# Moving the expert input products to even steps, regrouping the last steps' picks, and scattering the last three halves by quarters in a one-core Trainium2 kernel

## The reference, cut to what matters

```python
x = layernorm(x + attn(x))            # x: 4 x 1024 x 128, attn: gates and a scan over the sequence
# ffn, for all 4096 tokens; h = 8 heads, nk = 32 keys a side, k = 8, ne = 1024 experts
xn = (x - mu) * rsqrt(var + eps) * gamma + beta        # over the batch
q = xn @ w_q.T;  sim = einsum('pbnhd,hkpd->pbnhk', q, keys)
s, i = top_k(sim, 8)                                   # for x and for y
scores, pk = top_k(all pairs sx + sy, 8);  idx = take(ix * nk + iy, pk)
o = einsum('bnd,bnhkd->bnhk', inputs, key_in[idx])
o = gelu(o) * softmax(scores)
out = layernorm(x + einsum('bnhk,bnhkd->bnd', o, key_out[idx]))
```

## Time and profile before

| | |
|---|---|
| median of 3 runs | 500.65 us (500.22 to 504.22) |
| the profiled execution, in full | 502.43 us |
| its span, first to last instruction | 500.6 us |
| mean granted TensorE clock in it | 0.788 |
| DVE busy | 429.3 us (86%) |
| PE busy | 364.9 us (73%) |
| POOL busy | 255.0 us (51%) |
| ACT busy | 243.7 us (49%) |

### The profile page before, as it was taken

One profiled execution on the slowest core, in us unless ns is written; L12 is line 12 of the kernel. 1 busy time (PEld: TensorE's weight loads), 2 busy tenths in 40 slices (PEclk: granted clock), 3 DMA queues, 4 the chain that ended last, 5 costly groups with the idle time before them and its releaser, 6 DMA issues.

```text
span 500.6 us, 24184 instructions
## 1 busy us (share of the span) xinstructions
PE 364.9 (73%) x10097; PEld 266.1 (53%) x10097; DVE 429.3 (86%) x2691; ACT 243.7 (49%) x398; POOL 255.0 (51%) x345
## 2 busy tenths in 40 slices
PE   5979855266738787787877778778787778778755
PEld 3445542024433657375647554665467366737745
DVE  2457986999999889999999999999999999994922
ACT  2897664346324533563474437353654572344222
POOL 1023350552549465658747473769294938474600
PEclk9989956668556887887797679867987887878769
DMA  8800000000000000000000000000000000000001
GB/s 237 187 1 1 1 1 0 2 0 5 3 4 3 3 4 5 3 3 7 26 1 5 25 5 2 5 25 4 3 5 27 2 5 4 26 1 5 25 5 44
DMA packets 7662, 8.96 MB, mean 18 GB/s; under 512 B 896, under 2 KB 6912, under 8 KB 7424
## 3 DMA queue, kind: packets, MB, share of 16 engines
q1 hardware_dynamic: 6976, 7.34, 5.4%
q10 hardware_dynamic: 576, 0.07, 0.1%
HBM read 5.31 MB, written 2.10 MB: 15 GB/s over the span
## 4 chain that ended last, share of the span: by engine, by line
PE 39%; DVE 22%; issue 13%; POOL 10%; ACT 3%; ACTq 0%; DVEq 0%; POOLq 0%
PE psum L904 15%; PE psum L880 11%; PE psum L891 7%; PE psum L860 5%; DVE vals L625 4%; POOL arena L295 4%; DVE picked L658 3%; DVE idx L633 3%; DVE arena L689 3%; DVE arena L685 2%; POOL ixf L258 2%; DVE arena L682 2%; POOL code L263 1%; DVE top L639 1%; ACT arena L444 1%
## 5 line engine op out<-in xcount | busy, mean ns | idle before, releaser
L880 PE MATMUL psum<-arena 64*64 64x16 f16 x8192 | 93.6, 180 | 69.2 <-issue 60.9
L880 PEld LDWEIGHTS psum<-arena 64*64 64x64 f16 x8192 | 85.8, 116 | 87.7 <-issue 77.3
L904 PE MATMUL psum<-ko,arena 64*128 64x128 f32 x1024 | 90.4, 354 | 3.3 <-issue 3.3
L904 PEld LDWEIGHTS psum<-ko,arena 64*128 64x128 f32 x1024 | 87.0, 265 | 4.2 <-issue 3.8
L633 DVE FIND_INDEX8 idx<-vals,sims 128x8 uint32<-128x32 f32 x512 | 82.6, 186 | 0.0
L295 POOL TENSOR_TENSOR arena<-arena 128x512 f32<-128x512 f32 x60 | 77.3, 1318 | 4.8 <-ACT arena L436 4.8
L891 PE MATMUL psum<-x1T,trn 128*64 128x256 f32 x512 | 66.3, 412 | 13.8 <-ACT arena L444 13.7
L685 DVE TENSOR_TENSOR arena<-iota,listsT 128x4096 f16<-128x4096 f16 x32 | 76.3, 2385 | 0.0
L436 ACT ACTIVATE arena<-psum 128x1024 f32<-128x1024 f32 x32 | 32.6, 1018 | 67.8 <-PE psum L880 67.8
L891 PEld LDWEIGHTS psum<-x1T,trn 128*64 128x64 f32 x512 | 35.5, 148 | 51.5 <-ACT arena L444 25.8
L243 POOL TENSOR_TENSOR cand<-vals 128x128 f32<-128x128 f32 x16 | 9.4, 588 | 95.5 <-DVE vals L625 95.5
(11 more groups left out here) (118 smaller groups left out, 573.7 us busy)
## 6 DMA issues: line engine op xcount, KB each, us to landing
x<-in_L_attn_x_dram SPq DMA_DIRECT2D x8, 256.0 KB, 5.7
out_dram<-nat SPq DMA_DIRECT2D x7, 256.0 KB, 2.2
ko<-in_L_ffn_key_out_dram SPq DMA_DIRECT2D x2, 512.0 KB, 8.7
nat<-in_L_ffn_key_in_dram SPq DMA_DIRECT2D x2, 256.0 KB, 9.2
nat<-in_L_ffn_keys_dram SPq DMA_DIRECT2D x2, 128.0 KB, 5.6
out_dram<-nat SPq DMA_DIRECT2D x2, 128.0 KB, 1.7
nat<-in_L_attn_W_delta_dram SPq DMA_DIRECT2D x1, 64.0 KB, 2.9
nat<-in_L_attn_W_in_dram SPq DMA_DIRECT2D x1, 64.0 KB, 2.8
```

The source lines that it names most:

```text
L880: end = pe.matmul(psum[64 * e:64 * e + 64, at:at + NJ], hotx[rows, g, :, e], hotw[rows, part, g, :, e], start=(part == 0), stop=(part == 1))
L904: end = pe.matmul(y2[:, e, m % 2] if m < NS - 1 else y_last[:, e], gl[rows, m % 4, j, :], ko[rows, j, :], start=(j == 0), stop=(j == NJ - 1))
```

## The change

- `experts_in(q)` and `gelus(q)` run in step 2q and no longer in step 2q + 1 (`GELU_STEP`). In step 0 the Gelus stand ahead of `exps(0)`, `low_halves(0)` and `signs(0)`. In the other even steps `signs(m)` stands ahead of the third Gelu. The Gelu buffer `gl` has six slots for four.
- On DVE the `hots_of` of step 14 are taken out of step 15's body. After the loop stand `residual(5)`, `hots_of(14, 0)`, the statistics, the whole pick of step 15, `hots_of(14, 1)`, `hots_of(15, 0)`, `scales`, `hots_of(15, 1)`.
- The last three halves, (14, 1), (15, 0) and (15, 1), are scattered by `quarters`: 128 matmuls a half with 32 columns, the high and the low part side by side and no longer added in PSUM. ACT copies a quarter's low part out (`low_out`), DVE adds the high part (`both_parts`) and multiplies with the Gelus; for step 14's first half POOL does so in four short products after the last one-hots.
- `experts_out(13)` is issued before the last three halves.

```diff
+    GL = 6
+    GELU_STEP = tuple(range(0, NS, 2))
...
-        arena = sb("arena", [P, 24576])
+        arena = sb("arena", [P, 25600])
...
-        gl = arena[:, at_gl:at_gl + 4 * AW].rearrange("p (u j w) -> p u j w", u=4, j=NJ)
+        gl = arena[:, at_gl:at_gl + GL * AW].rearrange("p (u j w) -> p u j w", u=GL, j=NJ)
...
+        LAST = 2 * NS - 3
+        quarter_base = (0, 4, 2)
+
+        def quarter(u, part):
+            m, hf, b = (LAST + u // 2) // 2, (LAST + u // 2) % 2, u % 2
+            at = slice(32 * hf + 16 * b, 32 * hf + 16 * b + 16)
+            sums = psum[:, quarter_base[u % 3] * 512:(quarter_base[u % 3] + 2) * 512].rearrange(
+                "p (t g w j) -> p w j t g", t=2, g=16, w=2)
+            return sums[:, part], pn[:, m % 3].rearrange("p j (t g) -> p j t g", t=2)[:, :, :, at]
...
-            for m in range(NS + 1):
-                if m < NS:
-                    candidate_sums(m)
+            for m in range(NS):
+                candidate_sums(m)
                 if m >= 1:
                     weights(m - 1)
                 if m >= 3:
                     weigh(m - 3)
-                if m == NS:
-                    weigh(NS - 2)
-                if m < NS:
-                    candidate_codes(m)
-                    over_eighth(m)
+                candidate_codes(m)
+                over_eighth(m)
+            weigh(NS - 3)
+            weights(NS - 1)
+            pool.wait_ge(s["hot_done"], 2 * NS)
+            pool.wait_ge(s["p_evac"], LAST)
+            for r in range(4):
+                js = slice(4 * r, 4 * r + 4)
+                a = gl[:, (NS - 2) % GL, js].rearrange("p j (t g) -> p j t g", t=2)[:, :, :, 0:32]
+                pool.tensor_tensor(a, pn[:, (NS - 2) % 3, js].rearrange("p j (t g) -> p j t g", t=2)[:, :, :, 0:32], a,
+                                   ALU.mult).then_inc(s["a_done"], 1)
...
             def gelus(q):
-                wait(act, "y2_mm", q * 2 - 2)
+                wait(act, "y2_mm", q * 2 - 4)
                 for r in range(JR):
-                    if r == 2:
-                        signs(2 * q + 1)
+                    if r == 2 and q > 0:
+                        signs(GELU_STEP[q])
                     wait(act, "g_mm", q * JR + (r + 1))
...
+            sims_out(1)
+            normed(2)
+            gelus(0)
+            exps(0)
+            low_halves(0)
+            signs(0)
+            for m in range(1, NS):
+                high_copied(m - 1)
                 if m >= 2:
                     p_out(m - 2, 0)
-                if m < NS:
-                    exps(m)
-                if m >= 1:
-                    convert(m - 1)
-                if m < NS:
-                    low_halves(m)
-                if m >= 1:
-                    lists_out(m - 1)
+                exps(m)
+                convert(m - 1)
+                low_halves(m)
+                lists_out(m - 1)
                 if m >= 2:
                     p_out(m - 2, 1)
                 if m + 1 < NS:
                     sims_out(m + 1)
                 if m + 2 < NS:
                     normed(m + 2)
-                if m % 2 and m < NS:
-                    gelus(m // 2)
+                if m in GELU_STEP:
+                    gelus(GELU_STEP.index(m))
+                if m not in GELU_STEP:
+                    signs(m)
                 if m >= 5 and m % 2:
                     spread2(m // 2 - 2)
-                if m < NS and m % 2 == 0:
-                    signs(m)
                 if m >= 6 and m % 2 == 0:
                     norm_out(m // 2 - 3)
+            high_copied(NS - 1)
+            convert(NS - 1)
+            lists_out(NS - 1)
+            p_out(NS - 2, 0)
+            for u in range(6):
+                act.wait_ge(s["q_mm"], u + 1)
+                act.wait_ge(s["a_done"], (NS - 4 if u < 2 else NS - 3) * 4)
+                low, p = quarter(u, 1)
+                act.activation(p, low, ACT.Copy, scale=1.0 / W_SCALE).then_inc(s["low_out"], 1)
+                if u == 2:
+                    norm_out(NCH - 3)
...
-                wait(dve, "p_mm", m * 2 - 1 + hf)
+                if m * 2 + hf == 2 * NS - 1:
+                    dve.wait_ge(s["q_mm"], 2)
+                else:
+                    wait(dve, "p_mm", m * 2 - 1 + hf)
...
+                if 1 <= m < NS - 1:
                     hots_of(m - 1, 0)
                     if m >= 5 and m % 2:
                         residual(m // 2 - 2)
+                        stats(m // 2 - 2)
                     if m >= 6 and m % 2 == 0:
                         scales(m // 2 - 3)
                     hots_of(m - 1, 1)
+
+            dve.wait_ge(s["lists_evac"], NS - 1)
+            residual(NCH - 3)
+            hots_of(NS - 2, 0)
+            stats(NCH - 3)
+            pack(NS - 1)
+            pick(NS - 1)
+            sums_and_codes(NS - 1)
+            hots_of(NS - 2, 1)
+            hots_of(NS - 1, 0)
+            scales(NCH - 3)
+            hots_of(NS - 1, 1)
...
+            def both_parts(h):
+                m, hf = (LAST + h) // 2, (LAST + h) % 2
+                for b in range(2):
+                    u = 2 * h + b
+                    dve.wait_ge(s["low_out"], u + 1)
+                    high, p = quarter(u, 0)
+                    dve.scalar_tensor_tensor(out=p, in0=high, scalar=1.0 / W_SCALE, in1=p, op0=ALU.mult,
+                                             op1=ALU.add).then_inc(s["sum_done"], 1)
+                dve.wait_ge(s["sum_done"], 2 * h + 2)
+                at = slice(32 * hf, 32 * hf + 32)
+                a = gl[:, m % GL].rearrange("p j (t g) -> p j t g", t=2)[:, :, :, at]
+                dve.tensor_tensor(a, pn[:, m % 3].rearrange("p j (t g) -> p j t g", t=2)[:, :, :, at], a,
+                                  ALU.mult).then_inc(s["a_tail"], 1)
+
+            dve.wait_ge(s["gelu_done"], NCH * JR)
+            both_parts(0)
             residual(NCH - 2)
-            dve.wait_ge(s["gelu_done"], NCH * JR)
-            for hf in range(2):
-                if hf == 1:
-                    scales(NCH - 2)
-                dve.wait_ge(s["p_evac"], (NS - 1) * 2 + hf + 1)
-                at = slice(32 * hf, 32 * hf + 32)
-                a = gl[:, (NS - 1) % 4].rearrange("p j (t g) -> p j t g", t=2)[:, :, :, at]
-                dve.tensor_tensor(a, pn[:, (NS - 1) % 3].rearrange("p j (t g) -> p j t g", t=2)[:, :, :, at], a,
-                                  ALU.mult).then_inc(s["a_tail"], 1)
+            stats(NCH - 2)
+            both_parts(1)
+            both_parts(2)
+            scales(NCH - 2)
...
+            def quarters(m, hf):
+                h = m * 2 + hf - LAST
+                pe.wait_ge(s["hot_done"], m * 2 + hf + 1)
+                for b in range(2):
+                    u = 2 * h + b
+                    if u == 0:
+                        pe.wait_ge(s["sims_ready"], 2 * NS)
+                    elif u == 1:
+                        pe.wait_ge(s["gelu_done"], NCH * JR)
+                    elif u == 2:
+                        pe.wait_ge(s["p_evac"], LAST)
+                    else:
+                        pe.wait_ge(s["sum_done"], u - 2)
+                    for k in range(16):
+                        g = 32 * hf + 16 * b + k
+                        for e in range(2):
+                            for tile in range(2):
+                                rows = slice(64 * tile, 64 * tile + 64)
+                                at = (quarter_base[u % 3] + tile) * 512 + 2 * NJ * k
+                                end = pe.matmul(psum[64 * e:64 * e + 64, at:at + 2 * NJ], hotx[rows, g, :, e],
+                                                hotw[rows, :, g, :, e], start=True, stop=True)
+                    end.then_inc(s["q_mm"], 1)
...
+                if m >= NS - 2:
+                    pe.wait_ge(s["a_tail"], 1 if m == NS - 2 else 3)
                 for j in range(NJ):
                     if m < NS - 1:
                         wait(pe, "a_done", m * 4 + j // 4 + 1)
-                    else:
-                        pe.wait_ge(s["a_tail"], 2)
...
             scores(0)
-            for m in range(NS + 1):
-                if m == NS:
-                    lists_turned(NS - 1)
+            for m in range(NS):
                 if m >= 2:
                     scatter(m - 2, 1, 0, 12)
-                if 1 <= m < NS:
+                if m >= 1:
                     lists_turned(m - 1)
                 if m >= 2:
                     scatter(m - 2, 1, 12, 32)
                 if m + 1 < NS:
                     scores(m + 1)
-                if m % 2 and m < NS:
-                    experts_in(m // 2)
-                if m == NS:
-                    wait(pe, "lists_evac", NS)
-                    experts_out(NS - 3)
+                if m in GELU_STEP:
+                    experts_in(GELU_STEP.index(m))
+                if m == NS - 1:
+                    wait(pe, "lists_evac", m)
+                    experts_out(m - 3)
                 if m >= 1:
```

(14 more changed lines are left out.)

22 lines of the change are left out of this document (7 added, 15 removed).

## The result

The changed kernel takes 524.41 us (median of 4 runs, 523.25 to 525.26), the kernel before 502.02 us (4 runs, 500.22 to 504.22). The ratio is 1.0442 (95% interval 1.0386 to 1.0499): 4.4% slower. A run that comes out over 1.5% above the fastest of its kernel is left out of every ratio and interval here.

What follows compares the result with a forecast made beforehand. The prediction took DVE, busy 86% of the span, as the bound. Odd steps +27.0, old waits -7.5, step 0 +5.7 and tail -10.8 gave +14.4: 515 us against the median of 500.65, 8-in-10 range 503 to 525.

Steps and rivals of the forecast that it cites:

- the port: Even steps: POOL's SBUF reads and DVE's two-input one-hots exclude each other; an instruction takes 2.36 us instead of 0.31.
- The odd steps: Steps 5 to 15: DVE waits 4.5 us a step, between 3.5 and 6; six steps, +27.0 us.
- The 3.5 for ACT's queue: Odd steps: high copy done 8.47 us after the start, behind signs, Gelus and `norm_out`; DVE wants it at 4.98.
- the 0.4 for the clock: Odd steps: share taken of the 1.8 us by which products slow if PE's clock falls while idle.
- the 0.6 for the stalls: Odd steps: average for a 1.68 us stall in `experts_out` delaying the lists in two of six steps.
- a clock that stays low: Rival in the loop: PE drops to the lower rate in each even step's pause; 6.8 us a step, 529 us; chance 0.10.
- The old waits, -7.5: Loop from 161 us: DVE's waits for the high copy (4.2) and the turned lists (3.3) go, -7.5 us.
- Step 0, +5.7: Start: Gelus put first delay DVE's pack from 96.94 to 102.7 us; +5.7, at least 4, up to 8.
- The tail, -10.8: From step 15: its pick between step 14's one-hots -3.9, quarters -6.9; together -10.8 us, between -7 and -14.
- POOL gets ahead: Rival in even steps: `above` comes some 3 us earlier, odd steps wait 1.6 us each; 498 us; chance 0.12.
- even steps without waits: Rival in the loop: lighter even steps absorb the chain and the six odd-step waits are 0; 488 us; chance 0.10.
- the tail doesn't gain: Rival: the quarters' chain over ACT and DVE takes as long as the old scatter; 6.9 back, 522 us; chance 0.06.

Runs made afterwards that it cites:

- experiment 3: Changed kernel plus eight single-input statistics instructions between the one-hot halves of even steps from 4: 499.46 us; control with one two-input addition there: 535.34 us.
- experiment 1: Changed kernel with products back in odd steps and old step 0: 497.90 us; kernel before with moved Gelus, new step 0 order, old tail: 527.71 us.
- experiment 7: Experiment 1's first kernel with the old `scatter` instead of quarters for the last three halves: 507.69 us, ratio 1.0046 to the kernel before.
- experiments 2 and 6: 2: changed kernel with first products back in step 1, 517.83 us; 6: that plus half the next step's `greatest` between even steps' one-hots, 491.99 us.

## Why the prediction was right

The forecast was 515 us and slower by over 1%; measured were 524.4. The direction is right by its reason, the size is not: the range ended at 525, 0.6 away, and two of the four runs lie above it, so that the time fell inside is in part luck. The mechanism holds at each link: `above` 0.96 after the step, the signs at 1.0, the copy wanted 4.97 after the start (forecast 4.98), waits in all odd steps from 5 and in no even one, and the port as the reason (experiment 3). By its terms:

- **The odd steps: +37.2 for a forecast of +27.0.** This is the term that was mis-sized: 6.2 a step for 4.5, just beyond the 6 that the prediction gave as its upper bound. The 3.5 for ACT's queue is right: 3.42 where the clock held, 1.89 behind step 4, where the prediction forgot that no `norm_out` stands there yet. Wrong are the 0.4 for the clock and the 0.6 for the stalls, 1.0 a step together: in four of six steps the products were late by the clock, which by the first path alone is 8.6 / 6 = 1.4 us a step, and the lists took 9.6 / 6 = 1.6 more. The prediction had let the lists' lateness pass behind the high copy's, for "the two overlap and do not add"; the rows show both waits in five of the six steps, in step 9 3.42 and 3.44 one after the other. The prediction had a clock that stays low as a rival, at a chance of 0.10 with 6.8 a step and 529; with 6.2 the truth lay nearer to the rival. It had drawn from one row, step 3's 2.04 us of idle time ahead of products of 3.73 us, that the clock seldom falls. The rows after show 2.00 ahead of 5.36 us and 2.07 ahead of 3.73. A gap that goes well once isn't safe: more of the chance belonged on the clock.
- **The old waits, -7.5:** gone, and a further 1.1 us of DVE's steps with them.
- **Step 0, +5.7:** the wait is 5.80, the pack at 102.42 (forecast 102.7), and step 4 starts 5.5 later. The reading of ACT's queue, eight Gelus paced by PE, was exact.
- **The tail, -10.8:** -11.4, but by other shares, so that the sum fits is in part luck. Last one-hots to last products: 6.1 (6.3). Small waits: 2.01 for the lists (1.2), 2.09 for the slot (1.9). The one-hots of step 15 end 41.3 us plus the wait after the step's start (about 42). What was not seen: of the 11.4 some 5 us come because step 15 has no products to wait for, so the tail alone wins 6.7 (experiment 1), and the pick's new place nothing (experiment 7).
- **The other rivals:** "POOL gets ahead" and "even steps without waits" are refuted by each even step's `above`; "the tail doesn't gain" by experiments 1 and 7.
- **The stalls in the scatter.** The old halves keep theirs, 0.35 to 2.33 us each (five of them in experiment 7); the quarters have two for the same work, 1.80 and 0.28 in the changed kernel. By the ratios the quarters win 7.6 us, between 5 and 10. The prediction had 6.9 with the stalls. By the Trainium skill, "Runtime: NRT & Kernel Launch", section "Instruction fetch mechanics", which has the cost of a block of instructions mostly hidden, it would have been some 3 less; the runs do not agree with that. That the stalls are the loading of code is not shown here.

The profiled execution was forecast at 516.8 us and took 525.1: 8.3 more, which is +10.2 by the odd steps, -1.1 by the others, -0.2 by the start and -0.6 by the tail. The rows tie 8.6 us of the odd steps' waits to TensorE's clock; how the 9.6 of the lists divide between clock and stalls stays open.

## What to carry to other kernels

Where GpSimd's results sit on the critical path, look at what VectorE runs beside them: work with two SBUF inputs without a break lets GpSimd through about one instruction at a time (2.36 us for one of 0.31), and single-input work that is due anyway, put in between, lets it catch up at no cost (517.8 to 492.0 us here, ratios 1.0278 and 0.9721, experiments 2 and 6). Before moving a chain behind another in an engine's queue, count the lead that its first link has at that place, not the work in it. A move that leaves TensorE idle in the middle of a chain of matmuls should be charged for the lower clock with a good share of its full price (four of six paid here), even where one row shows a gap that did no harm.

## What the runs showed of the hardware

- The hold between VectorE and GpSimd goes both ways: a code instruction of 0.31 us takes 2.36 beside one-hots, and one-hots of 2.3 take 3.36 beside `weigh`, whose four instructions take 8.50 there and 4.96 ahead of the one-hots.
- Beside DVE work with one SBUF input POOL is not held: its instructions of 0.31 stay 0.31 beside the residual, BN_STATS and MAX8 (16 MAX8 take 1.57 us with POOL's codes beside them and without).
- After idle gaps of 2.00 to 4.07 us, 32 listed matmuls took 5.34 to 6.67 us in four cases; after 1.68 and 2.07 they took 3.73. Filling the gap with 60 matmuls gave 3.73 in step 6 and made the kernel 2.3% faster. The length of the gap alone doesn't tell which it will be.
- A kernel can become 5% faster by more work of the right kind in the right place (experiment 3).
